# Retention layers with a mixture of experts beside them: first layer reordered, tile turns from the ninth step, parts_gate's wait split

## The reference

```python
def block(h, p):                       # scanned over L = 4 layers
    r = _retention(h, wk)
    m = r @ w1 + b1
    a, gate = jnp.split(m, 2, axis=-1)
    m = a * jax.nn.silu(gate) @ w2 + b2
    m = _groupnorm1(m, gg, gb)
    y = m + h
    f = jax.nn.gelu(y @ wf1 + bf1_, approximate=False) @ wf2 + bf2_
    return (_layernorm(f + y, lg, lb), None)

def _L0_ffn_ref(x, gate_w, w1, b1, w2, b2):
    expert_idx = jnp.argmax(jax.nn.softmax(x_flat @ gate_w, axis=-1), axis=-1)
    for e in range(NUM_EXPERTS):       # 8 experts, each token keeps one of them
        h = jax.nn.gelu(x_flat @ w1[e] + b1[e], approximate=False)
        out = out + jnp.where(expert_idx == e, expert_w, 0.0)[:, None] * (h @ w2[e] + b2[e])

xn = _layernorm(x, axis=-1)            # x is (8, 512, 128) in float32
x = x + _L0_attn_ref(xn, ...) * _silu(_L0_ffn_ref(xn, ...))
```

## Time and profile before

| | |
|---|---|
| time, median of 3 runs | 481.32 us (480.12 to 483.1) |
| the profiled execution's own time | 483.59 us |
| its span | 481.8 us |
| TensorE busy | 465.3 us, 97% of the span |
| VectorE busy | 360.2 us, 75% |
| ScalarE and GpSimd busy | 264.9 and 265.0 us, 55% each |

### The profile page before, as it was taken

One profiled execution on the slowest core, in us unless ns is written; L12 is line 12 of the kernel. 1 busy time (PEld: TensorE's weight loads), 2 busy tenths in 40 slices (PEclk: granted clock), 3 DMA queues, 4 the chain that ended last, 5 costly groups with the idle time before them and its releaser, 6 DMA issues.

```text
span 481.8 us, 9903 instructions
## 1 busy us (share of the span) xinstructions
PE 465.3 (97%) x3149; PEld 392.0 (81%) x3149; DVE 360.2 (75%) x1306; ACT 264.9 (55%) x562; POOL 265.0 (55%) x303
## 2 busy tenths in 40 slices
PE   6999999999999999999999999999999999999994
PEld 5897767777889889898889898898898897877664
DVE  4857787778878766777766777677777677786897
ACT  3924444444565545664446664455664456659673
POOL 4453788886454555444455444654544655654792
PEclk9979999999999999999999999999999999999999
DMA  9999910012511111110111111120111110044145
GB/s 262 251 143 178 381 36 29 33 35 77 109 63 40 45 62 62 62 44 35 40 62 62 61 46 61 39 68 29 62 45 59 41 40 7 5 125 86 22 44 89
DMA packets 47394, 36.63 MB, mean 76 GB/s; under 512 B 13336, under 2 KB 38752, under 8 KB 47312
## 3 DMA queue, kind: packets, MB, share of 16 engines
q1 hardware_dynamic: 41232, 28.93, 22.9%
q0 software_dynamic: 5440, 6.28, 5.9%
q10 hardware_dynamic: 672, 0.79, 0.5%
HBM read 16.27 MB, written 10.99 MB: 57 GB/s over the span
## 4 chain that ended last, share of the span: by engine, by line
PE 77%; DVE 9%; POOL 7%; issue 3%; ACT 2%; DMA 1%; SPq 0%; DVEq 0%; POOLq 0%
PE bank L1775 10%; PE bank L1656 7%; PE bank L1640 7%; PE pair L1863 5%; PE bank L1877 5%; PE pair L1854 4%; PE pair L1820 4%; POOL x_slots L560 4%; PE bank L1685 4%; PE pair L1865 4%; PE bank L1687 4%; PE bank L1686 4%; PE pair L1815 3%; PE bank L1741 2%; PE bank L1773 2%
## 5 line engine op out<-in xcount | busy, mean ns | idle before, releaser
L632 POOL TENSOR_TENSOR zhat<-zhat,all_lg 128x512 f32<-128x512 f32 x28 | 37.5, 1341 | 81.8 <-PE bank L1731 75.5
L1775 PE MATMUL bank<-all_f,G_sb 128*128 128x128 f32 x512 | 72.9, 275 | 0.0
L1775 PEld LDWEIGHTS bank<-all_f,G_sb 128*128 128x128 f32 x512 | 67.4, 192 | 1.7 <-issue 1.7
L889 ACT ACTIVATE y_sb<-bank,gn_bi,gn_sc 128x512 f32<-128x512 f32 x29 | 22.6, 778 | 80.6 <-DVE gn_bi L1475 80.6
L862 ACT ACTIVATE uT_h<-bank 128x512 fp32r<-128x512 f32 x30 | 17.9, 597 | 84.9 <-PE bank L1741 80.5
L1640 PEld LDWEIGHTS bank<-moe_w,h_T 128*128 128x128 f32 x312 | 39.5, 191 | 13.8 <-issue 13.8
L480 POOL TENSOR_TENSOR ln_rs<-ln_ve,half_neg 128x4 f32<-128x4 f32 x31 | 32.8, 1059 | 28.9 <-DVE ln_ve L1003 28.6
L759 ACT ACTIVATE h_T<-bank,w_t 128x128 f32<-128x128 f32 x156 | 44.5, 372 | 5.1 <-PE bank L1656 5.1
L683 POOL DMA_INDIRECT y_rows<-yt,slot_info x39 | 40.8, 1045 | 11.1 <-POOL yt L680 11.1
L819 ACT ACTIVATE G_sb<-bank,all_par 128x512 f32<-128x512 f32 x62 | 41.4, 694 | 5.5 <-PE bank L1713 3.1
L1656 PE MATMUL bank<-xtT,w_t 128*128 128x128 f32 x312 | 43.3, 282 | 0.0
(11 more groups left out here) (229 smaller groups left out, 1232.5 us busy)
## 6 DMA issues: line engine op xcount, KB each, us to landing
w_t<-moe_w SPq DMA_DIRECT2D x39, 258.0 KB
x_slots<-moe_w SPq DMA_DIRECT2D x1, 2515.5 KB, 20.7
xt<-x_slots SPq DMA_DIRECT2D x39, 64.0 KB, 1.8
x_sb<-in_L_attn_x SPq DMA_DIRECT2D x8, 256.0 KB, 5.8
moe_w<-in_L_ffn_w SPq DMA_DIRECT2D x1, 2048.0 KB
moe_w<-y_rows SPq DMA_DIRECT2D x8, 256.0 KB, 4.3
out<-in_L_attn_x SPq DMA_DIRECT2D x1, 1536.0 KB
out<-moe_w POOLq DMA_DIRECT2D x6, 256.0 KB, 4.4
```

The source lines that it names most:

```text
L1775: last = mm(dst, G_sb[:, k, at_c], all_f2[:, n // B, k, :], start=False, stop=k == 1)
```

## The change

It has six parts.

1. **Turns.** PLACES starts in step 8 instead of 7 and leaves out only the EARLY place of step 15. Step 7 has no turn any more, step 8 has turns 0 and 1 instead of turn 2, step 22 has two turns instead of one; from the LATE place of step 22 on all is as before. Step 8 stays not parted, step 22 becomes parted.
2. **Scatters.** The numbers in SCATTERS change: steps 2 to 7 have 10, 5, 5, 5, 6, 1 instead of 9, 7, 6, 6, 4, 0. The splits of the later layers' first weights on GpSimd go from step 7 to the ends of steps 7, 8 and 9.
3. **VectorE's z_hat** of steps 2 to 6 goes from the end of its step to behind the mask of the next.
4. **find_experts** goes from the end of step 2 to behind its group sums, where VectorE waits for the means. In steps 1 to 6 the layer norm's statistics (L993) go ahead of split_u.
5. **TensorE's zhat_by_feature** goes behind outputs in the first layer.
6. **parts_gate**, in all steps, waits for uT_h alone ahead of its first two products and for uT_l ahead of the third.

```diff
--- before.py
+++ after.py
@@ -266,8 +266,7 @@
 
 
         EARLY, LATE = range(2)
-        PLACES = [(s, place) for s in range(B - 1, LB) for place in (EARLY, LATE)
-                  if not (place == EARLY and s in (B, B + 7, B + 14))][:TURNS]
+        PLACES = [(s, place) for s in range(B, LB) for place in (EARLY, LATE) if (s, place) != (2 * B - 1, EARLY)][:TURNS]
         assert len(PLACES) == TURNS
 
         def turn(l, t, place):
@@ -286,7 +285,7 @@
         def parted(l, t):
 
 
-            return turn(l, t, EARLY) is not None and l > 0
+            return (turn(l, t, EARLY) or 0) > 0 and l > 0
 
         def parted_steps(l, t):
 
@@ -509,7 +508,7 @@
             pool.wait_ge(ln_in, 32)
 
 
-            SCATTERS = {2: (5, 1, 3), 3: (2, 2, 3), 4: (1, 2, 3), 5: (1, 2, 3), 6: (1, 2, 1)}
+            SCATTERS = {2: (5, 1, 4), 3: (1, 1, 3), 4: (1, 1, 3), 5: (1, 1, 3), 6: (1, 2, 3), 7: (1, 0, 0)}
             assert sum(map(sum, SCATTERS.values())) == NT
 
             def choose_expert():
@@ -653,9 +652,6 @@
                 if first and t == 1:
                     count_tokens()
                 scatter(l, t, 0)
-                if first and t == B - 1:
-                    for k in range(1, L - 1):
-                        split_f1(k)
                 tile_rows(l, t, LATE)
                 if s >= 1:
                     gn_pow(s - 1)
@@ -664,9 +660,9 @@
                 scatter(l, t, 1)
                 if s >= 2:
                     ln_pow(s - 2, s % B)
-                if first and t == B - 1:
-                    split_f1(L - 1)
                 scatter(l, t, 2)
+                if B - 1 <= s < B + L - 2:
+                    split_f1(s - B + 2)
 
             def tile_rows(l, t, place):
 
@@ -1352,6 +1348,8 @@
                     mask(s)
                 if first and t == 2:
                     find_slots()
+                if first and t > 2:
+                    z_hat(l, t - 1)
                 if s:
                     gate_tanh(s - 1)
                 if not first:
@@ -1365,6 +1363,8 @@
                     normalise_u(s)
                 if 1 <= s < NO_TILES:
                     group_sums(s - 1)
+                if first and t == 2:
+                    find_experts()
 
                 if first:
                     tile_in(l, t, EARLY)
@@ -1373,9 +1373,9 @@
                 tile_out(l, t, LATE)
                 if s == NO_TILES:
                     return
-                for stage in (gn_moments, split_u) if first and 1 <= t < B - 1 else (split_u, gn_moments):
+                for stage in ((gn_moments, z_stats, split_u) if first and 1 <= t < B - 1 else
+                              (split_u, gn_moments, z_stats)):
                     stage(l, t)
-                z_stats(l, t)
                 gn_shift(l, t)
                 z_moments(l, t)
                 tile_in(l, t, LATE)
@@ -1385,12 +1385,11 @@
                 y_residual(l, t)
                 if first and t == 1:
                     add_rank()
-                if first and t == 2:
-                    find_experts()
                 if first and t == B - 2:
                     later_biases()
                 tile_expert(l + (t + 1) // B, (t + 1) % B, EARLY)
-                z_hat(l, t)
+                if not (first and 2 <= t < B - 1):
+                    z_hat(l, t)
 
             def ending():
 
@@ -1821,11 +1820,15 @@
 
             def parts_gate(n):
 
-                pe.wait_ge(uT_split, n + 1)
+                w = all_w[:, n // B]
+                pe.wait_ge(uT_done, n + 1)
                 if n % B == 0:
                     pe.wait_ge(part_made, parts_made("w", n // B))
                 need(pe, gn_chain, gn_steps(n - 1, 1) if n else 0)
-                parts_product(bank[3], all_w[:, n // B], slice(D, 2 * D), uT_h, uT_l, pe_g)
+                mm(bank[3][:, :], w[:, 0, D:2 * D], uT_h[:, :], start=True, stop=False)
+                mm(bank[3][:, :], w[:, 1, D:2 * D], uT_h[:, :], start=False, stop=False)
+                pe.wait_ge(uT_split, n + 1)
+                mm(bank[3][:, :], w[:, 0, D:2 * D], uT_l[:, :], start=False, stop=True).then_inc(pe_g, 1)
 
             def parts_value(n):
 
@@ -1913,9 +1916,12 @@
                     zhat_by_feature(l, t)
                 gelu_first(l, t, 0)
                 gelu_first(l, t, 1)
+                if first:
+                    outputs(s)
                 if not parted(l, t):
                     zhat_by_feature(l, t)
-                outputs(s)
+                if not first:
+                    outputs(s)
                 second_weight(s - 1)
                 if first and t == 1:
                     pe.wait_ge(rows_done, 1)
```

## The result

The changed kernel takes 484.36 us (median of 9 runs, 482.7 to 487.18), the kernel before 481.53 beside it (9 runs, 479.95 to 483.1). The ratio of the runs is 1.0059 with a 95% interval of 1.0035 to 1.0082: **slower by 0.6%**, where I had forecast faster by 0.7%. The profiled execution took 487.18, with a span of 485.4 against 481.8.

What follows compares the result with a forecast made beforehand. TensorE was taken as the bound from step 8 on, with first-layer stalls from VectorE. 1.20 + 0.42 + 0.50 + 0.50 + 2.27 + 0.23 - 1.64 = 3.48 off 481.32 gives 477.8 us, range 475.5 to 480.4.

Steps and rivals of the forecast that it cites:

- Step 8: Loses tile_back, gains one transposition (12.39), plus a 0.55 stall of scores for q_sb: 12.94 us instead of 13.17, gain 0.23.
- the forecast's 3.48: Total gain in us summed over steps 3 to 8, less the loss in step 22.
- Tile 0: Last scatter out at 115.3, SyncE's xt starts at 117.6, lands at 119.4; TensorE wants it at 120.3, spare 0.9.
- The rival built on it: Tile 0 comes late behind step 7's rows_scale and rows_shift, stalling TensorE; 482.9 us with 6 us of delay; chance 0.05.
- Steps 4 to 6: First layer, VectorE's z_hat no longer delays sums and mask: gains of 0.42, 0.50 and 0.50 us, steps near 12.0.
- Step 3: First layer, stalls of 1.48 us behind find_experts and z_hat go, less a new 0.25: gain 1.20, step at 12.2.
- Step 7: Loses both turns: 12.0 us instead of 14.27, gain 2.27, after adding 0.7 for second_weight and u_sb, 0.1 for parts_gate.
- Step 22: Gets two turns and becomes like step 9: 14.81 us instead of 13.17, 1.64 lost.
- The steps from 9 on: Steps 9 to 21 and 23 on keep their products and lengths, 350 us taken as fixed; otherwise the prediction fails.
- the stalls did not vanish: Rival: waits left in the forecast, 2.25 us in steps 3 to 8, go half or wholly; 475.6 us; chance 0.18.
- GpSimd did not pace the changed kernel: Rival: GpSimd's powers stay late, steps 4 to 6 keep their length, 1.42 us lost; 479.3 us; chance 0.17.
- My slower side: Slower than before through tile 0 arriving late, chance 0.05; slower by over 1% needs over 8 us late or a mishap, 0.03.

Runs made afterwards that it cites:

- warm_8: Changed kernel with six products that nobody reads put on TensorE in step 8, behind tile 0's transposition; 483.14 us, ratio 1.0043.
- old_turns_2: Changed kernel with before's turns, all splits at the end of GpSimd's step 7, and 6, 5, 6, 6 scatters in steps 3 to 6; 482.31 us, ratio 1.0020.
- after_again: The changed kernel run a second time, word for word; 484.59 us, ratio 1.0053 to the kernel before.
- mended_2: Changed kernel; step 8: early xtT copy, gelu_first's bank 3 half first; one scatter moved from step 2 to 3, all splits ending step 7; 480.0 us, 0.9960.
- old_turns: Changed kernel with the turns, parted steps and scatters of the kernel before; 480.81 us, ratio 0.9973.
- turns_only: Kernel before with part 1 (turns) alone; 486.88 us, ratio 1.0132.
- skip_8e: Changed kernel with the left-out EARLY turn in step 8 instead of step 15; 483.65 us, ratio 1.0043.

## Why the prediction was wrong

**Step 8 is the step that failed.** The prediction said: "But a wait appears: scores need q_sb", and from it "step 8 lasts 12.94, gain 0.23". That wait came to about 0.3 and was the small one. I had added one transposition at 0.11 and asked only whether its input, xt, would land in time. I did not ask who must read its output before the bank is written again. The runs showed in its place a wait of 2.56 ahead of gelu_first for VectorE's copy out of bank 4, and a clock at 0.50 behind it: 19.31 instead of 12.94. The row was to be had: in every later step with a turn in the EARLY place, step 9 for one, gelu_first takes its halves in the other order, because they are parted. Step 8 became the only whole step behind the first layer with such a turn; the new line on parted makes it so. The forecast's sentence that a whole step 8 costs "13.17 - 0.89 + 0.11" treats it as the sum of pieces from two kinds of steps, neither of which has this pair of neighbours. The clock was no term at all. Without it step 8 would have been 16.4 (warm_8), 3.5 over the forecast, and that alone would have eaten the forecast's 3.48.

**Tile 0** was right to 0.2: last scatter at 115.42 (115.3), SyncE's xt at 117.78 (117.6), the transposition at 120.33 (120.3) with no wait. Those rows:

```profile
115.42 1.01 POOL L559 DMA_INDIRECT x_slots<-xn,pos  x1 [0.15 <-issue]
...
117.78 0.34 SPq L416 DMA_DIRECT2D xt<-x_slots  x1
```

The rival built on it was right in kind, as old_turns_2 shows, and did not take place in this kernel.

**Steps 4 to 6** came out right (-0.49, -0.56, -0.63 for -0.42, -0.50, -0.50), partly by luck: half of it comes with parts 2, 4 and 6, which I had put at nothing; the scatter less per step that I took as needed to keep up is a gain of its own, and the order gives only 0.27 to 0.39. **Step 3** gave 0.47 instead of 1.20. find_experts does no harm any more, but the means waited 0.57 for a gs that GpSimd's rows_shift held up; after_again and mended_2 show 14.28 and 12.75 for that step, so that no single number was to be had. **Step 7** gave 2.48 (2.27): the 0.7 that I added for second_weight and u_sb was too much. In the timeline second_weight starts 0.13 and u_by_feature 0.34 late. **Step 22** is exact at 14.81.

**The steps from 9 on** I had taken as fixed, and named that as what the prediction stands on. Four of them grew, by 0.73 in all. Step 10 grew by the splits, which I had looked at only for GpSimd's own time: it is 14.80 to 14.82 wherever no split runs beside it. For step 9 the splits are enough with the turns of before (14.99 in old_turns, 14.81 in old_turns_2), but with the changed turns they are not the whole cause: turns_only lasts 14.96 there, has no split in that step, and its ln_nb starts 0.15 late. In 12 and 24 ln_nb also starts late, by 0.25 and 0.2, although GpSimd's ln_rs is on time. Step 12 is 15.04 to 15.06 long in each kernel with the changed turns (14.80 in skip_8e) and 14.80 to 14.81 with those of before; the cause is open.

**The rivals**: the stalls did not vanish. GpSimd did not pace the changed kernel, but with before's scatters it holds steps 5 and 6 up by 0.3 each (old_turns), so that rival was not empty. My slower side had a chance of 0.05 by one mechanism; the one that came was not on the list.

## What to carry to other kernels

When a step gets a combination of pieces that no step had before, don't price it as a sum of known steps: list for each piece which bank or buffer it writes, who must empty it, and what stands ahead of that reader on its engine. And a stall like this one of 2.6 us is to be priced twice, at its length and at what the products behind it take at half clock (here 0 to 2.9 us more, 1.2 by the medians); the second part comes in some executions and not in others. Moving a piece of work on GpSimd is not free because GpSimd has time: look at which short VectorE instructions it will now run beside.
